# The second attention's score maxima computed with four 32-row tiles in four PSUM banks, and the separated keys dropped

## The reference, cut to what matters

```
x = x + cross_attention_0(layernorm(x), ctx)   # 8 heads of 64, context of 154 tokens
x = x + moe_0(layernorm(x))                    # 16 experts, top 4, one shared expert
x = x + cross_attention_1(layernorm(x), ctx)   # 16 heads of 8, context of 154 tokens
x = x + moe_1(layernorm(x))                    # 8 experts, top 2, shared expert

# cross_attention_1, for batch b and head h (2 batches, 512 tokens each, 154 context tokens):
q = x @ Wq;  k = ctx @ Wk;  v = ctx @ Wv       # width 8 for each head
scores  = q @ k.T / sqrt(8)                    # 512 x 154 for each head
weights = softmax(scores, axis=-1)
out     = concat_over_heads(weights @ v) @ Wo
```

## Time and profile before

| what | value |
|---|---|
| median of three runs | 231.21 us (231.13 to 231.42) |
| profiled execution, first to last instruction (span) | 229.8 us |
| PE busy | 223.2 us (97%), 1389 matmuls |
| DVE busy | 163.5 us (71%) |
| ACT busy | 155.3 us (68%) |
| POOL busy | 126.4 us (55%) |
| share of the chain that ended last: PE, ACT, DVE | 83%, 6%, 3% |
| granted TensorE clock, mean | 1.000 |

### The profile page before, as it was taken

How to read it: one execution, slowest core, us unless ns; L and a number is a source line. 1 busy time by engine, 2 the same in 40 slices (tenths; PEclk the granted TensorE clock), 3 DMA queues, 4 the chain that set the end, 5 groups by cost and what they waited for, 6 DMA issues and landing times.

```text
span 229.8 us, 4648 instructions
## 1 busy us (share of the span) xinstructions
PE 223.2 (97%) x1389; PEld 166.4 (72%) x1389; DVE 163.5 (71%) x480; ACT 155.3 (68%) x378; POOL 126.4 (55%) x127
## 2 busy tenths in 40 slices
PE   7999999999999999999999999999999999999994
PEld 3576765974989898889535563588878887888873
DVE  3689984788667953699948983564857776776874
ACT  2589999986678446662689788876365686645561
POOL 2766742898057927856592107209499400996540
PEclk9999999999999999999999999999999999999999
DMA  6890000000038924800600000037000003600002
GB/s 208 198 303 8 0 3 0 0 3 1 3 93 230 365 105 165 203 0 4 219 3 0 7 0 6 0 82 287 3 0 0 1 3 105 265 0 4 1 0 91
DMA packets 10174, 17.07 MB, mean 74 GB/s; under 512 B 3715, under 2 KB 5540, under 8 KB 9766
## 3 DMA queue, kind: packets, MB, share of 16 engines
q1 hardware_dynamic: 9926, 16.45, 23.1%
q10 hardware_dynamic: 224, 0.32, 0.4%
HBM read 16.08 MB, written 0.62 MB: 73 GB/s over the span
## 4 chain that ended last, share of the span: by engine, by line
PE 83%; ACT 6%; DVE 3%; DMA 2%; SPq 2%; POOL 2%; issue 1%; DVEq 0%; POOLq 0%
PE psum L1170 12%; PE psum L1173 11%; PE psum L1171 11%; PE psum L1326 7%; ACT prob L748 5%; PE psum L1384 5%; PE psum L1333 4%; PE psum L1335 3%; PE psum L1334 3%; PE psum L1435 3%; PE psum L1278 3%; PE psum L1288 3%; PE psum L1404 2%; PE psum L1256 2%; PE psum L1245 2%; DMA ctxT<-in_ctxT 2%
## 5 line engine op out<-in xcount | busy, mean ns | idle before, releaser
L702 POOL TENSOR_TENSOR act_s<-act_s,spread 128x512 f32<-128x512 f32 x35 | 44.4, 1292 | 19.8 <-DMA spread<-cw 13.6
L1170 PE MATMUL psum<-xT_hi,w_hi 128*128 128x512 f32 x108 | 43.9, 406 | 0.0
L1173 PE MATMUL psum<-xT_lo,w_hi 128*128 128x512 f32 x108 | 42.2, 391 | 0.0
L1171 PE MATMUL psum<-xT_hi,w_lo 128*128 128x512 f32 x108 | 42.2, 391 | 0.0
L797 ACT CAST q<-psum 128x512 fp32r<-128x512 f32 x35 | 20.4, 586 | 20.3 <-PE psum L1335 13.7
L1006 DVE TENSOR_TENSOR q<-psum,q 128x512 fp32r<-128x512 f32 x35 | 23.8, 687 | 13.3 <-ACT q L797 13.0
L787 ACT ACTIVATE act_s<-psum 128x512 f32<-128x512 f32 x39 | 23.0, 597 | 12.3 <-PE psum L1173 7.9
L1143 DVE TENSOR_REDUCE neg_max<-psum 128x2 f32<-128x308 f32 x64 | 26.2, 471 | 4.9 <-PE psum L1384 4.7
L702 POOL TENSOR_TENSOR hid<-hid,spread 128x512 f32<-128x512 f32 x13 | 16.6, 1297 | 18.9 <-DMA spread<-cw 14.6
L652 POOL TENSOR_TENSOR rstd<-vareps,minus_half 128x4 f32<-128x4 f32 x8 | 8.1, 1014 | 33.9 <-DVE vareps L907 33.9
L646 POOL TENSOR_TENSOR w_lo<-w_src,w_hi 128x768 fp32r<-128x768 f32 x12 | 21.7, 1830 | 8.9 <-ACT w_hi L717 8.9
(11 more groups left out here) (171 smaller groups left out, 468.2 us busy)
## 6 DMA issues: line engine op xcount, KB each, us to landing
spread<-cw SPq DMA_DIRECT2D x16, 256.0 KB, 4.4
spread<-cw SPq DMA_DIRECT2D x6, 512.0 KB, 5.5
w_src<-in_w SPq DMA_DIRECT2D x2, 1152.0 KB, 5.3
w_src<-in_w SPq DMA_DIRECT2D x1, 2304.0 KB, 12.4
spread<-cw SPq DMA_DIRECT2D x8, 128.0 KB, 2.9
w<-in_w SPq DMA_DIRECT2D x1, 576.0 KB, 6.9
out<-X SPq DMA_DIRECT2D x4, 128.0 KB, 1.8
wv<-in_wv SPq DMA_DIRECT2D x2, 192.0 KB, 4.8
```

Source lines behind the costliest of these rows:

```text
L702: pool.tensor_tensor(g, g, spread[:, slot, :], ALU.mult).then_inc(weighed, 1)
L1170: pe.matmul(dst, w_hi, xT_hi[:, b, :], start=True, stop=False)
L1171: pe.matmul(dst, w_lo, xT_hi[:, b, :], start=False, stop=False)
L1173: return pe.matmul(dst, w_hi, xT_lo[:, b, :], start=False, stop=True)
```

## The change

The scores for the maxima become 12 PE steps `score1(b, h, c)`. The eight pairs of group and token block of a set are cut into parts of 3, 3 and 2 (`PEAKS`). A step waits until four banks are free and then issues, for each pair, four matmuls: head j's 32 rows of `q1` against head j's 32 rows of the keys, 128 x 154, into bank number j of the four (3 or 2 times 154 columns of each bank). DVE has 48 steps `peak(b, h, c, j)` in place of its 64 reductions: one over a bank, of 3 x 154 or 2 x 154 values. Since each head now has its own rows of the array, the copies with zeroed rows aren't needed: `k1` is what `k_stack` was, for all four groups, `place_k1` is gone with its waits, and `expT` and `place_k1s` read `k1`.

The order of all other steps is the same on every engine. All bank numbers are given anew, in the first MoE, the first attention and the second MoE too: the bank that has been free longest, in the order of the steps.

```diff
+PEAKS = ((0, 3), (3, 6), (6, 8))
...
-    steps += [("place_k1", g, j) for g in groups for j in range(4)]
...
-    steps += [("score1", b, t, g, half) for b in batches for h in range(2) for t in range(T) for g in REST_SETS[h] for half in range(2)]
+    steps += [("score1", b, h, c) for b in batches for h in range(2) for c in range(len(PEAKS))]
+    steps += [("peak", b, h, c, j) for b in batches for h in range(2) for c in range(len(PEAKS)) for j in range(4)]
...
-        "scores.0.4 vf.3 q.1 q.2 scores.3.5 scores.6.1 vs.7 pT.2 scores.7.0 pT.4 q.3 pT.2 q.5 pT.6 scores.1.4 " +
+        "scores.4.6 vf.7 q.0 q.1 scores.5.3 scores.2.7 vs.0 pT.1 scores.4.6 pT.0 q.5 pT.1 q.3 pT.2 scores.0.7 " +
...
+        "h3.4 h1.6 qd.1 down down q1.0.2.7.1 down h3.6 score1.3.4.0.2 h1.7 score1.1.3.4.7 h1.0 down h3.6 " +
+        "score1.2.1.0.3 down h3.4 h3.7 mT.2 down score1.6.1.0.3 down down expT.2.4 score1.7.6.1.0 expT.3.5 " +
+        "expR.2 expR.4 expT.3.7 xT.6 score1.2.1.0.4 rest1.2.5 qd.1 mT.3 expT.6.7 pv1 q1.0.4.3.6 pv1 expR.1 " +
+        "score1.7.0.4.3 expR.6 expT.1.7 expT.6.0 score1.4.3.1.7 rest1 score1.6.0.4.3 pv1 expT.1.7 oT.6 mT.0 " +
+        "expT.2.4 score1.3.1.7.0 score1.2.4.3.6 pv1 expR.1 oT.7 expT.0.2 expT.5.4 score1.1.3.6.0 onT.2 expT.7.5 " +
+        "expR.1 wo1.3 mT.6 wo1.2 rest1.0.1 expT.6.3 pv1 expR.4 expR.7 pv1 expT.2.5 xT.6 expT.3.4 rest1 expT.7.2 " +
...
-                k1 = sb("k1", [P, B, G1, 4, CTX], F32R, r2)
+                k1 = sb("k1", [P, G1, B, CP], F32R, r2)
...
-                    k_stack = sb("k_stack", [P, 2, B * CP], F32R, r3)
...
-                    act.mul(k1[:, :, g, j, :], k[:, :, 0:CTX], head_rows[:, j:j + 1]).then_inc(k1_placed, 1)
...
-                    moved(dve.tensor_reduce(neg_max1[:, b, g // 2, 2 * half:2 * half + 2, g % 2, t],
-                                            bank(step)[:, 0:2 * CTX].rearrange("p (j c) -> p j c", j=2), AX, ALU.max, negate=True),
-                          step)
+                elif kind == "peak":
+                    b, h, c, j = step[1:]
+                    lo, hi = PEAKS[c]
+                    key = ("score1",) + step[1:]
+                    wait_filled(dve, key)
+                    moved(dve.tensor_reduce(neg_max1[:, b, h, j, lo:hi],
+                                            bank(key)[:, 0:(hi - lo) * CTX].rearrange("p (i c) -> p i c", i=hi - lo), AX, ALU.max,
+                                            negate=True), key)
...
-                    filled(pe.matmul(bank(step)[:, 0:2 * CTX].rearrange("p (j c) -> p j c", j=2), q1[:, b, g, t * P:(t + 1) * P],
-                                     k1[:, b, g, 2 * half:2 * half + 2, 0:CTX], start=True, stop=True), step)
+                    b, h, c = step[1:]
+                    keys = [step + (j,) for j in range(4)]
+                    for key in keys:
+                        wait_bank_free(pe, key)
+                    lo, hi = PEAKS[c]
+                    for n in range(lo, hi):
+                        g, t = REST_SETS[h][n // T], n % T
+                        wait_moved(pe, ("q1", b, g))
+                        wait_moved(pe, ("k1", g))
+                        for j, key in enumerate(keys):
+                            rows = slice(PAD * j, PAD * j + PAD)
+                            ins = pe.matmul(bank(key)[:, (n - lo) * CTX:(n - lo + 1) * CTX], q1[rows, b, g, t * P:(t + 1) * P],
+                                            k1[rows, g, b, 0:CTX], start=True, stop=True, skip_group_check=True,
+                                            tile_position=(PAD * j, 0))
+                            if n == hi - 1:
+                                filled(ins, key)
...
-                        filled(pe.matmul(bank(key), k1[rows, b, g, j, 0:P], q1[rows, b, g, :], start=True, stop=True,
+                        filled(pe.matmul(bank(key), k1[rows, g, b, 0:P], q1[rows, b, g, :], start=True, stop=True,
```

More of the change, by code:

```diff
@@ L152 @@
     "PE":
[24 rows of a table removed]
-    "ACT":
-        "kT split lnB kT xT kT kT lnB q xT q split " + 16 * "score " +
-        "pT score score pT k1 pT score pT score score split score pv pv score pv pv place_k1 score score " +
-        "score score score split score score place_k1 pT score score place_k1 lnB pT k1 pT xT split k1 pT " +
[3 rows of a table removed]
[L184 to L190, removed]
@@ L191 @@
-    "DVE":
[L192 to L205, removed]
@@ L206 @@
-    "Pool":
[L207 to L210, removed]
[20 rows of a table added]
+    "ACT":
+        "kT split lnB kT xT kT kT lnB q xT q split score score score score score score score score score score " +
+        "score score score score score score pT score score pT k1 pT score pT score score split score pv pv " +
+        "score pv pv score score score score score split score score pT score score lnB pT k1 pT xT split k1 pT " +
+        "gate split k1 pv pv pv pv h1 cwT h1 h1 h1 lnB xT h1 gate h1 h1 h1 h1 h1 cwT split split h1 h1 lnB h1 h1 " +
+        "xT h1 qd split h1 q1copy q1copy q1copy q1copy split h1 split split h1 mT exp exp exp expR lnB expR xT " +
+        "exp exp exp qd mT exp exp q1copy q1copy q1copy q1copy expR expR exp exp exp exp split split od exp exp " +
+        "mT exp exp split od expR exp exp exp onT expR mT exp exp exp exp exp expR lnB expR exp xT exp exp exp " +
+        "exp exp exp exp od route od h1 cwT h1 h1 h1 hsplit hsplit h1 onT h1 h1 h1 h1 h1 h1 hsplit hsplit hsplit " +
+        "hsplit lnB h1 hsplit xT h1 hsplit hsplit h1 h1 h1 h1 hsplit h1 hsplit h1 hsplit hsplit h1 hsplit hsplit " +
+        "route hsplit h1 h1 cwT hsplit h1 h1 hsplit hsplit h1 hsplit h1 ycopy hsplit hsplit ycopy h1 hsplit h1 " +
+        "h1 hsplit h1 hsplit h1 hsplit hsplit h1 hsplit hsplit h1 hsplit h1 hsplit hsplit h1 hsplit hsplit h1 " +
+        "hsplit ycopy ycopy ",
@@ new lines @@
+    "DVE":
+        "lnA sel lnA xT vf1 q q vf xT score score score score score score score score score norm score vf q q " +
+        "score norm score vs score pT score score pT norm score q q pT norm score pT score pT pT score k1 pT " +
+        "score pT score score norm score score score score score score score score norm pT wo pT norm wo score " +
+        "lnA score pT norm pT vf1 pT k1 pT xT pT pT gate route route route route wo wo lnA k1 h3 vs1 xT k1 gate " +
+        "h3 h3 route h3 route h3 route h3 h3 h3 route h3 h3 res lnA xT h3 h3 qd h3 h3 peak peak peak h3 peak " +
+        "peak peak peak peak peak h3 peak peak peak h3 h3 peak peak peak peak res lnA peak peak peak peak peak " +
+        "peak xT peak peak qd peak peak peak peak peak peak peak peak peak peak peak peak peak oT peak peak peak " +
+        "peak peak peak peak oT peak peak peak peak wo1 wo1 lnA xT gate route route oT oT h3 h3 hsplit hsplit h3 " +
+        "wo1 h3 wo1 hsplit h3 h3 lnA hsplit h3 hsplit hsplit hsplit xT h3 h3 gate hsplit hsplit route h3 h3 " +
+        "hsplit h3 hsplit h3 hsplit h3 hsplit h3 h3 hsplit hsplit route hsplit h3 h3 h3 hsplit hsplit h3 hsplit " +
+        "hsplit h3 h3 hsplit h3 h3 hsplit hsplit h3 h3 h3 hsplit h3 hsplit hsplit hsplit h3 h3 hsplit h3 h3 " +
+        "hsplit hsplit h3 hsplit hsplit h3 hsplit h3 hsplit hsplit h3 res res res res last_res last_res ",
@@ new lines @@
+    "Pool":
+        "lnA split lnA bo bo split norm norm norm norm norm norm norm lnA norm place_k1s split split split lnA " +
+        "place_k1s weigh weigh weigh weigh weigh weigh weigh weigh split split lnA weigh weigh weigh weigh weigh " +
+        "weigh weigh weigh split split lnA split place_k1s place_k1s split split split lnA split split weigh " +
+        "weigh weigh weigh weigh lnA weigh weigh weigh weigh weigh weigh weigh weigh weigh weigh weigh weigh " +
+        "weigh weigh weigh weigh weigh weigh weigh weigh weigh weigh weigh weigh weigh weigh weigh ",
@@ L211 @@
     "SP":
-        "store spread spread spread spread spread fetch store spread spread spread spread spread place_max " +
-        "fetch place_max place_max place_max store spread spread spread spread spread store spread spread " +
-        "spread spread spread out out out out ",
+        "store spread spread spread spread spread fetch store spread spread spread spread spread place_max fetch " +
+        "place_max place_max place_max store spread spread spread spread spread store spread spread spread " +
@@ L215 @@
+        "spread spread out out out out ",
 }
@@ L221, in takes @@
     if engine == "PE":
-        return True
-    if kind in ("scores", "q1", "expT"):
+        return kind != "peak"
+    if kind in ("scores", "q1", "expT", "score1"):
         return False
@@ L260, in bank_uses @@
             keys = [step[:3] + (2 * step[3] + j,) for j in range(2)]
+        elif kind == "score1":
+            keys = [step + (j,) for j in range(4)]
         elif kind == "pv1":
@@ L810, in _ @@
                     act.copy(rounded[:, g % 2, 0:B * CP], bank(step)[:, 0:B * CP]).then_inc(k1_rounded, 1)
-                elif kind == "place_k1":
```

(34 more changed lines are left out.)

8 lines of the change are left out of this document (3 added, 5 removed), and 39 rows, old and new, of the table PROGRAM.

## The result

| | us | granted clock |
|---|---|---|
| before, median of 4 (231.13 to 231.86) | 231.31 | 1.000 |
| changed, median of 4 (246.11 to 247.39) | 246.83 | 0.936 |
| changed, profiled execution (span) | 245.6 | 0.936 |

A forecast was written before the change was run, and what follows sets the result against it. PE was taken to bound the kernel, busy 97%, with DVE close behind. PE's and DVE's savings are consumed by waits of 0.6 + 0.8 + 0.8 + 0.15 + 1.8 = 4.15, so 231.2 + 4.1 = 235.3 us, range 233.6 to 239.0.

The forecast's parts named there:

- PE's price: Second attention's scores on PE: 64 matmuls of about 9.0 us become steps of 0.50 and 0.37, 5.5 us; 3.5 relieved.
- R: Time of one round of four 32-row score matmuls of 154 columns on PE: 0.13 us, ends 0.11 and 0.26.
- Rival A: Narrow score tiles on PE stream at the upper price, 0.26 us a round: 238.8 us; chance 0.20.
- DVE's price: Reductions of 462 values spaced 0.54 us, of 308 values 0.39; DVE saves 0.3 a set, 1.1 in all.
- rival B: Banks come free in time, PE's relief counts between 97 and 136 us, DVE's 1.1 comes off: 230.1 us; chance 0.13.
- Item 1: First attention, PE near 20.6 us: the second step of matmuls waits for a bank ACT reads; +0.6 us.
- Item 2: Batch 0's first score set: first score at 98.0, later steps wait for banks, `res` at 110.2; +0.8 us.
- Items 3 to 5: Batch 0's second set and batch 1's two sets: waits for banks, DVE and exponentials; +0.8, +0.15 and +1.8 us.
- Item 5's `oT` wait: Batch 1, second set: DVE's first `oT` of batch 0 comes late, the score step needs its bank; PE stands some 1.7 us.
- From `wo1` PE works on without a gap worth naming, so the shift stays: After `wo1`, forecast at 139.25 instead of 135.69, PE has no notable gap and the delay carries to the end.
- The sign on ACT: The sixteen copies of keys are gone from ACT and its busy time falls by some 8 us.
- The sign that I named for the forecast: PE has idle time in 97 to 140 us, released by DVE's maxima and ACT, several us where it had 0.8.

The follow-up runs named there:

- fill_all: The changed kernel with 32 useless matmuls of 512 columns filling TensorE's waits at eight places: 238.95 us, ratio 1.029.
- fill_early: The changed kernel with 12 useless matmuls in three waits alone, at 101, 113.9 and 115.4 us: 241.59 us, ratio 1.043.
- order_fill: The changed kernel with score steps and maxima at other places, banks dealt by when they are read, and 16 useless matmuls in five waits: 234.32 us, ratio 1.012.
- quads_order: The changed kernel with score steps cut to one head and one bank each, at other places, banks dealt by when they are read: 235.16 us, ratio 1.016.
- before_gap: The kernel before, with TensorE made to wait once at a score step near 112 us for a weight transfer: 235.94 us, ratio 1.016.
- quads: The changed kernel with each score step cut in four, one head and one bank each, same places and banks: 244.87 us, ratio 1.057.

## Why the prediction was wrong

The step that failed is the one ahead of the sum: "the granted clock is 1.00 throughout" was read from the kernel before and carried to the changed one, and every wait was priced at its own length. PE's idle time was forecast, to several us; that idle time would change the speed of all that PE does behind it stood in no term and in no rival. Filling took 7.9 of the 15.5 us off the measured time, and at the first `pv1` 9.0 of 15.0: that is the clock's. At most 5.9 is left there for the waits, against 4.15 forecast, so the waits were undercounted as well, by less than 2 us.

- PE's price: right. R = 0.12 (0.13 taken); a step 0.50 and 0.38. Rival A (R = 0.26) is out, and what it would have explained, a long time with slow rounds, was not the reason.
- DVE's price: right, 0.55 for 0.54, 0.1 us a set. The saving was added up wrongly: four times 6.24 - 5.88 is 1.4, not 1.1; the reductions' busy time fell by 1.3 (26.2 to 24.9). The forecast doesn't use it, rival B does.
- Item 1, the first attention's banks: 0.6 forecast, 0.1 measured, q of batch 0 at 95.66 against 95.57. The wait at 20.6 us was short: the vs step behind it starts at 21.46 against 21.24, 0.2 late.
- Item 2: `res` at 110.97, +1.55 against 109.42 where +0.8 was forecast. The first step stood at 98.59, not 98.0, behind a `down` that had waited 0.43 for DVE's h3 product and an h3 after it; its first maximum came at 99.19, not 98.7. The second step's wait of 1.07 for a bank stood at 101.14, where the forecast had 99.9; ahead of the third no wait shows.
- Items 3 to 5: with the clock held (fill_all) `rest1` is at 117.56, +2.8 against 114.78, forecast 1.8 (116.6; its signs say 1.9), and `wo1` at 141.71, +6.0 against 135.69, forecast 3.55 without item 1. The filling's own cost is in the second of these, and fill_early, which fills nothing behind 115.6 us and keeps the clock until 135, tells some of it: a score step stands at 132.85 there and at 132.87 in fill_all, the next at 135.24 and 135.44. So it is 0.2 us up to there; the last four useless matmuls (138.80 to 139.94) can add up to 1.1.
- Item 5's `oT` wait was there, 1.79 us, but it was not a term that could be taken away: without it the exponential came second, 0.84, and the time stayed. The sum adds the waits as if each went when its cause went.
- "From `wo1` PE works on without a gap worth naming, so the shift stays": the shift is 13.6 us at `wo1`, where the clock was still at half (until 152.3 and a little more), and 15.0 at 153.43. From there it stays at 15.0 to PE's last matmuls. The rest of the span's 15.8 stands behind them, where the four output transfers land after 2.7 us instead of 1.8.
- The sign on ACT: its busy time fell by 5.8 us (155.3 to 149.5), not by some 8.
- Rival B fell with the waits. The sign that I named for the forecast, idle time released by DVE and ACT, was met; I gave no sign on the clock.

The Trainium skill describes such a kernel in "TensorE: Matmul & The Clock Gate", "A second HAM failure mode: psum-queue depth-cycling": one that cycles through PSUM banks idles TensorE briefly and often, and its clock swings between the two levels. This trace agrees, with 0.99, 0.50, 0.99 and 0.50 in four successive stretches, and waits of 0.4 to 1.0 us ahead of the two falls. It would have been a rival with the right sign; the section gives no price.

What stays open: which pattern of waits lowers the clock and which leaves it; where fill_all's wait at 207 us comes from; and whether the new matmuls can beat the kernel before with a better order. With the clock held, order_fill is 2.7 us above it and the best execution of quads_order 2.0 above the fastest of before beside it (233.4 against 231.4). PE's saving of 3.5 us was never seen as time. A likely reason, which no run shows, is DVE: it was busy for 90% of the first and last stage before, and had nearly as much to do as ever.

## What to carry to other kernels

In this kernel, with TensorE 97% busy, the full clock hung on that fullness: before trading instructions for waits, ask what the waits do to the speed of all that follows, and price them at more than their length. Read the granted clock by stretches of every new profile before any wait is explained; when it falls, fill the waits with useless matmuls once, which separates the clock from the waits in one run. Ask of a saving on a full engine whether its nearly full partner can follow. And place a step that takes several banks where their readers come next, not where its inputs are ready: other places and banks alone gave 5.6 us here.

## What the runs showed of the hardware that was not expected

- What stood ahead of a fall to half clock: in the changed kernel waits of 0.98 and 0.92 us with 0.5 of work between, in fill_early one of 1.80, in before_gap one of 3.00. One of 1.07 in the changed kernel, and 0.52, 0.35 and 0.91 in fill_early, were followed by none. In before_gap the clock then stays at half for 4.8 us in which PE is fully busy.
- Executions of one program differ in time as they differ in clock: quads_order took 233.4, 233.8, 236.6 and 236.7 us at 1.000, 0.993, 0.985 and 0.978. One execution of the kernel before had 0.990 and took 233.1 instead of 231.4.
- Row tiles overlap even when they are issued head after head, three matmuls in a row on the same 32 rows (quads). Twelve matmuls take 0.66 until the next step; one behind the other, at the 0.12 of a round, they would take 1.4:

```profile
98.65 0.74 PE L1371 MATMUL psum<-k,q 32*128 32x154 f32 x12
99.31 0.50 PE L1153 MATMUL psum<-xT_hi,w_hi 128*128 128x512 f32 x1
```

The Trainium skill ("TensorE: Matmul & The Clock Gate", "The mechanism") states that matmuls start and end strictly in their order. Then the next head's first could not start ahead of this head's third, and four heads would take more than 4 x 2 x 0.12 = 0.96, if each head's three follow each other at that distance. The measured 0.66 is less, and the starts of these twelve show heads that pass each other (the matmuls of L1371 alone and their weight loads; in brackets how many have started):

```profile
98.60:98.70 0.10, 0.05 (x3) 0.06 (x3) 1.00 0.00 0
98.60:98.90 0.30, 0.25 (x7) 0.26 (x10) 1.00 0.00 0
```

By 98.70 three matmuls have started and by 98.90 seven; in strict order, with 0.12 between two on the same rows, it would be one and at most four. Page and measurement differ, and the measurement decides: in this trace matmuls of different row tiles did not start in their order.
